# Macaron block on one Trainium2 core: the first batch's attention operands are prepared inside the first expert mixture

## The chip, the cores and the metric

The kernel runs on one NeuronCore of a Trainium2 chip, in one launch. The metric is the device time of that core in microseconds (us). SyncE (SP) and the DMA queues move data, TensorE (PE) multiplies, VectorE (DVE), ScalarE (ACT) and GpSimd (POOL) do the rest. Each engine runs its own instructions in order and waits on semaphores.

## What is computed

Four batches of 1024 rows of 128 floats pass through a feed-forward mixture, an attention and the same mixture again:

```python
x = L0_attn_x                                   # (4, 1024, 128)
x = x + 0.5 * ffn(layernorm(x))                 # first mixture
x = x + attn(layernorm(x))                      # 16 heads of 8, per batch
x = x + 0.5 * ffn(layernorm(x))                 # second mixture

# ffn: layernorm, router logits (8 experts), top 2, softmax gates, then per expert
x1 = x @ W1 + b1                                # 128 -> 512
x2 = clip(x @ W2 + b2, -20, 20)
hidden = clip(x1 * (x2 * sigmoid(x2)), -1e4, 1e4)
y = clip(hidden @ Wo + bo, -1e4, 1e4)           # 512 -> 128, summed over the 2 experts by gate
# attn: q = k = v = x @ W_qkv.T; softmax(q q^T / sqrt(8)) q; @ W_o.T
```

## The kernel before

**Mixtures.** Routing (`*_route`) ranks the experts of each row and scatters the normalised rows by expert into DRAM (`rows_dram`); the rows of an expert lie there in the order of the batches. A mixture then walks over 40 blocks: 32 "pairs" of 256 rows and at the end 8 "singles" of 128 rows, which take what is left of each expert. `vector_lay_out_early` finds the expert and the first row of blocks 0 to 16, which need the first three batches alone, `vector_lay_out_late` those of blocks 17 to 39. For every block SP loads the expert's 776 KB record of weights (`sync_load_record`, L837) and the block's rows (`sync_load_rows`, L842) into one of six slots. PE turns the rows (L1914), multiplies four chunks by W2 and W1 (L1959, L1961), DVE clips (L1689), ACT takes the Silu (L1281), DVE multiplies (L1700) and clips the whole `hidden` (L1708), PE makes the second product (L1971), ACT adds the bias (L1290), DVE clips (L1715), PE turns back (L1981), ACT weighs by the gate (L1299) and POOL scatters the result to `y_dram` (L1143). A block's steps are laid among the chunks of the next ones: in `tensor_experts` the second product of block i-1 stands between chunk 2 and chunk 3 of block i. A block's load waits until the results of the block six before are scattered (`sync_next_block`). After block 5 (first mixture) or 13 (second) SP writes eight filler rows (`sync_fillers`, L807).

**Between the first mixture and the attention.** Only when all results are scattered does SP load the first batch's results (L849, into `first_mixed`); then a table `PREPARED` of chores runs on all engines: DVE adds them to x (L1803), takes statistics (L1426, L1429), POOL the power (L1156), DVE normalises (L1818), PE turns (L2112), multiplies by W_qkv (L2118) and turns q into values (L2125), ACT copies from PSUM (L1360, L1370), DVE splits q into three bf16 parts (L1827 to L1833), SP writes them to `q_dram` (L894), SP and ACT load them as operands of the first team of four heads (L942, L1316). POOL blanks the zero parts of the operand tiles of all three operand sets and of the two value tiles in the same stretch (L1041 to L1051).

```python
PREPARED = [("prepare", 0, k, (h, 2)) for k, h in ((0, 0), (1, 0), (0, 1), (1, 1), (2, 0), (2, 1))]
```

**Attention.** Sixteen turns, one for each team of four heads of a batch. PE first makes 26 units of row-maximum scores (`tensor_row_max`, L2024, L2025; DVE reduces each, L1753). From there slots of scores (`tensor_scores`, L2043 to L2049), exponentials (ACT, L1326) and values (L2067) run, with a table `chores` that sets which other piece is issued behind which slot. Before the first score the negative row maxima must have gone through POOL (`pool_place`, L1058), DRAM (L974) and back into the right operand (L982): the chore "place" on SP, which in `sync_attention` stands behind the rows of ones of operand sets 1 and 2 (L902), the 22 loads of the second team (L942, L948, L923) and the load of batch 1's results (L883). Preparing batches 1 to 3 and the second routing are chores of the slots.

**Second mixture.** Like the first; a table `TAIL` puts the last of the attention and of the routing among its first blocks. At the end all results are loaded (`last_y`), added (L1725) and written.

## Time and profile before

| | us |
|---|---|
| median of 3 runs (1425.15 to 1428.48) | 1428.48 |
| the profiled execution, as timed | 1427.73 |
| its span, first to last instruction | 1426.0 |
| PE busy in the span | 1248.9 (88%) |
| DVE busy | 1170.2 (82%) |
| ACT busy | 896.2 (63%) |
| POOL busy | 511.2 (36%) |
| mean granted clock of TensorE | 0.964 |

The program's stages in the trace: routing to 108 us, first mixture to 331, preparing to 371, attention to 1166 (its last pieces among the second mixture's first blocks), second mixture to 1404, last sums to 1426. The busy shares are means over these stages; a stage has to be read by itself. The granted clock is given as a share of full speed: 1.0 is 2.4 GHz, 0.5 is 1.2 GHz.

### The profile page before, as it was taken

How to read it: one execution, taken by the hardware profiler on the slowest of the kernel's cores; microseconds unless marked ns; L12 is line 12 of the kernel's file. 1: busy time of each engine (PE TensorE's matmuls, PEld its weight loads, DVE VectorE, ACT ScalarE, POOL GpSimd, SP SyncE). 2: the span in 40 equal slices, each digit the busy share in tenths (PEclk: the TensorE clock that was granted, in tenths of full speed). 3: DMA queues.
4: the chain of work that ended last, by engine and by line, in shares of the span. 5: the costliest groups of instructions: out<-in, count | busy, mean ns of one | idle time of the engine just before them, and what ended most of it. 6: DMA issues, size and time to landing. Idle time of an engine off the chain costs nothing.

```text
span 1426.0 us, 29423 instructions
## 1 busy us (share of the span) xinstructions
PE 1248.9 (88%) x10053; PEld 649.7 (46%) x10053; DVE 1170.2 (82%) x2305; ACT 896.2 (63%) x1876; POOL 511.2 (36%) x595
## 2 busy tenths in 40 slices
PE   3738999984389999999999999999999988889992
PEld 3727888872022222322323323233322247778882
DVE  8876788876698899889898988988899458868885
ACT  1214555552058888888778887788877865545651
POOL 3875333334433000243335324351434023433331
PEclk9999999996589999999999999999999999999997
DMA  8126545451311201102111011011101312445555
GB/s 260 38 71 217 203 180 191 178 204 34 104 51 35 72 19 35 36 24 66 36 40 48 17 57 36 17 52 36 36 3 32 113 62 101 161 170 186 188 204 192
DMA packets 65382, 135.58 MB, mean 95 GB/s; under 512 B 13330, under 2 KB 34932, under 8 KB 65204
## 3 DMA queue, kind: packets, MB, share of 16 engines
q1 hardware_dynamic: 56196, 116.18, 23.7%
q0 software_dynamic: 8704, 16.93, 3.7%
q8 instruction: 83, 1.36, 0.4%
q14 instruction: 63, 0.52, 0.1%
q10 hardware_dynamic: 336, 0.59, 0.1%
HBM read 47.35 MB, written 25.07 MB: 51 GB/s over the span
## 4 chain that ended last, share of the span: by engine, by line
PE 44%; DVE 21%; DMA 3%; issue 3%; ACT 3%; SPq 1%; POOL 0%; ACTq 0%; POOLq 0%; DVEq 0%
PE psum L2067 13%; DVE att_neg_part L1753 11%; PE psum L2043 7%; PE psum L2047 5%; PE psum L2024 5%; PE psum L1971 3%; PE psum L1959 3%; PE psum L1961 3%; DVE att_neg_part L1758 2%; DVE stats L1426 1%; ACT att_probs L1326 1%; DMA y_dram<-ffn_y,ffn_block_rows 1%; PE psum L2090 1%; ACT att_o_t L1341 1%; DMA ffn_rec<-record 1%
## 5 line engine op out<-in xcount | busy, mean ns | idle before, releaser
L1326 ACT ACTIVATE att_probs<-psum 128x512 f32<-128x512 f32 x1024 | 556.5, 596 | 119.3 <-PE psum L2049 90.3
L1753 DVE TENSOR_REDUCE att_neg_part<-psum 128x2 f32<-128x1024 f32 x441 | 532.0, 1223 | 69.0 <-PE psum L2025 56.0
L2067 PE MATMUL psum<-att_probs,att_values 128*16 128x256 f32 x4096 | 321.4, 386 | 6.3 <-ACT att_o_t L1341 4.2
L1281 ACT ACTIVATE ffn_silu<-ffn_x2c,ffn_rec 128x256 f32<-128x256 f32 (+1 forms) x320 | 154.6, 487 | 163.3 <-DVE ffn_x2c L1689 162.6
L1143 POOL DMA_INDIRECT y_dram<-ffn_y,ffn_block_rows x144 | 142.1, 987 | 274.5 <-ACT ffn_y L1299 248.7
L2024 PE MATMUL psum<-att_right,att_left 64*128 64x512 bf16 x512 | 198.3, 388 | 27.5 <-DMA att_right<-q_parts_dram 15.9
L2043 PE MATMUL psum<-att_right,att_left 64*128 64x512 bf16 x512 | 198.6, 388 | 4.9 <-DVE att_neg_part L1753 4.8
L2046 PE MATMUL psum<-att_right,att_left 64*128 64x512 bf16 x512 | 198.5, 388 | 4.0 <-DVE att_neg_part L1753 2.1
L1689 DVE TENSOR_SCALAR ffn_x2c<-psum,ffn_rec 128x256 f32<-128x256 f32 (+1 forms) x320 | 162.8, 513 | 45.9 <-PE psum L1961 41.7
L2025 PE MATMUL psum<-att_right,att_left 64*128 64x512 bf16 x512 | 198.9, 389 | 0.0
L2047 PE MATMUL psum<-att_right,att_left 64*128 64x512 bf16 x512 | 193.7, 378 | 0.0
L2049 PE MATMUL psum<-att_right,att_left 64*128 64x512 bf16 x512 | 193.4, 378 | 0.0
L1959 PE MATMUL psum<-ffn_block_t,ffn_rec 128*128 128x256 f32 (+1 forms) x640 | 179.4, 362 | 1.3 <-ACT ffn_block_t L1239 1.1
L1961 PE MATMUL psum<-ffn_block_t,ffn_rec 128*128 128x256 f32 (+1 forms) x640 | 178.6, 361 | 0.0
L2067 PEld LDWEIGHTS psum<-att_probs,att_values 128*16 128x16 f32 x4096 | 68.1, 94 | 223.0 <-issue 125.3
L1700 DVE SCALAR_TENSOR_TENSOR ffn_hidden<-psum,ffn_rec,ffn_silu 128x256 f32<-128x256 f32 (+1 forms) x320 | 144.5, 452 | 18.9 <-ACT ffn_silu L1281 16.7
L1971 PE MATMUL psum<-ffn_hidden,ffn_rec 128*128 128x256 f32 (+1 forms) x640 | 142.6, 366 | 13.6 <-DVE ffn_hidden L1708 13.5
L1127 POOL DMA_INDIRECT rows_dram<-rows,place_i x128 | 128.5, 1004 | 72.4 <-issue 36.8
L1058 POOL TENSOR_TENSOR att_max_rest<-att_max_rest,att_max_parts 16x128 f32<-16x128 f32 x64 | 26.7, 417 | 337.4 <-ACT att_max_parts L1381 334.8
L2043 PEld LDWEIGHTS psum<-att_right,att_left 64*128 64x128 bf16 x512 | 47.4, 93 | 197.2 <-ACT att_probs L1326 125.6
L1971 PEld LDWEIGHTS psum<-ffn_hidden,ffn_rec 128*128 128x128 f32 x640 | 113.9, 193 | 32.5 <-DVE ffn_hidden L1708 18.8
L1961 PEld LDWEIGHTS psum<-ffn_block_t,ffn_rec 128*128 128x128 f32 x640 | 117.9, 192 | 13.7
(198 smaller groups left out, 1514.4 us busy)
## 6 DMA issues: line engine op xcount, KB each, us to landing
ffn_rec<-record SPq DMA_DIRECT2D x80, 776.5 KB, 3.7
ffn_block_rows<-rows_dram SPq DMA_DIRECT2D x64, 130.0 KB, 2.2
att_left<-q_parts_dram SPq DMA_DIRECT2D x64, 96.0 KB
att_right<-q_parts_dram SPq DMA_DIRECT2D x120, 48.0 KB
record<-in_L_ffn_W SPq DMA_DIRECT2D x16, 256.0 KB, 6.5
last_y<-y_dram SPq DMA_DIRECT2D x8, 512.0 KB, 7.4
att_right<-q_parts_dram SPq DMA_DIRECT2D x90, 32.0 KB
y_dram<-ffn_y,ffn_block_rows POOLq DMA_INDIRECT x144, 2.6
```

The source lines that it names most:

```text
L1326: S.activation(probs[:, slot % PROBS, :], ring_bank(("score", slot))[:, :], ACT.Exp, scale=SCALE).then_inc(att_bank.by_act, 1)
L1753: last = V.tensor_reduce(out=neg_part[:, h % 2, keys, p::PAIR, t], in_=psum[:, low:high + 1, :], axis=AX.X, op=ALU.max, negate=True)
L1959: TE.matmul(both[:, few], rec[:, s, W2 + c * P:W2 + (c + 1) * P], block_t[:, m % 2, few], start=True, stop=True)
L1961: TE.matmul(both[:, w1_few], rec[:, s, W1 + c * P:W1 + (c + 1) * P], block_t[:, m % 2, few], start=True, stop=True).then_inc(chunked, 1)
L1971: last = TE.matmul(y_bank[n % 2][:, few], rec[:, s, WO + c * F:WO + (c + 1) * F], hidden[:, n % 2, c, few], start=(c == 0), stop=(c == HC ...
L2024: TE.matmul(bank[low], left[s][TOP, p, q], right[s][TOP, p, k], start=True, stop=True)
L2025: TE.matmul(bank[high], left[s][BOTTOM, PAIR + p, q], right[s][BOTTOM, PAIR + p, k], start=True, stop=True).then_inc(maxed, 1)
L2043: TE.matmul(low, left[s][TOP, p, k], right[s][TOP, p, q], start=True, stop=False)
L2046: TE.matmul(high, left[s][BOTTOM, PAIR + p, k], right[s][BOTTOM, PAIR + p, q], start=True, stop=False)
L2047: TE.matmul(low, left[s][TOP, PAIR + p, k], right[s][TOP, PAIR + p, q], start=False, stop=True).then_inc(att_bank.filled, 1)
L2049: TE.matmul(high, left[s][BOTTOM, p, k], right[s][BOTTOM, p, q], start=False, stop=True).then_inc(att_bank.filled, 1)
L2067: last = TE.matmul(value_bank[head * VS:head * VS + VW, q], values[:, b % 2, kt, team * TEAM + head, :], probs[:, (UNIT * n + j) % PROBS, ...
```

## The change

The blocks of both mixtures are put in another order: pairs 0 to 22, then the eight singles (23 to 30), then nine pairs (31 to 39). Within each section the layout now lists first those blocks that hold rows of the first batch and then the others (16 columns of expert and half in place of 8), so that the first batch's results are complete with block 30. The layout has more small DVE instructions, and the ones over blocks are twice as wide.

In the first mixture a new table `HEAD` puts the preparing of the first batch among blocks 33 to 38, and six blanking chores among blocks 8 to 13. `plan_head(block, slots)` counts four slots to a block:

```diff
+        plan_head(BEGIN, [(HC * n, "blank", n, 0) for n in range(6)])
+        plan_head(SINGLES.stop, [
+            (8, "begin", 0, "load"), (12, "begin", 0, "add"), (13, "begin", 0, "statistics"),
+            (14, "begin", 1, "add first"), (15, "begin", 1, "add second"),
+            (16, "begin", 0, "power"), (16, "begin", 1, "statistics"), (17, "begin", 0, "normal"),
...
-        PREPARED = [("prepare", 0, k, (h, 2)) for k, h in ((0, 0), (1, 0), (0, 1), (1, 1), (2, 0), (2, 1))]
...
         def sync_next_block(k, i):
-            n = k * BLOCKS + i - SLOTS
-
-            Q.wait_ge(scattered_y[n % YSETS], y_scatters(n + 1, n % YSETS))
+            Q.wait_ge(biased, k * BLOCKS + i - SLOTS[k] + 1)
+            sync_load_record(k, i)
+            if i >= ROW_SLOTS:
+                n = k * BLOCKS + i - ROW_SLOTS
+                Q.wait_ge(scattered_y[n % YSETS], y_scatters(n + 1, n % YSETS))
             sync_load_rows(k, i)
-            sync_load_record(k, i)
+
+        def sync_first_team():
+
+            sync_ones(0)
+            sync_write_parts(0, 0)
+            sync_operand_lefts(0)
+            for n in FIRST_RIGHTS:
+                Q.dma_start(*right_load(0, n)).then_inc(first_pair_in, 16)
+            sync_write_parts(0, 1)
...
             G.wait_ge(combined, HC * BLOCKS)
             for r in range(YSETS):
                 G.wait_ge(scattered_y[r], y_scatters(BLOCKS, r))
-            pool_blank_values(0)
-            pool_blank_left(0)
-            for chore in PREPARED:
-                pool_chore(*chore)
-            pool_blank_right(0)
-            G.wait_ge(split_done, 1)
-            pool_blank_values(1)
             for s in range(1, OPERANDS):
-                pool_blank_left(s)
-                pool_blank_right(s)
+                for n in range(4):
+                    pool_blank_operands(s, n)
```

The work of the preparing is dealt out anew: POOL adds and normalises half 0, DVE half 1; ACT loads the results (`first_mixed`) and makes the three casts of each half, DVE only the subtractions; PE uses the value bank of PSUM one piece after another. SP writes the parts and loads the first team's first operands in `sync_first_team`, behind its last block load; ACT loads the others at the start of the attention. The blanking of the values and of operand set 0 is now in blocks 8 to 13, that of sets 1 and 2 stays behind the mixture. The first mixture has four record slots and the second six, both six row slots; a record waits for the bias of the block that had its slot, the rows still for the scattering of the block six before, and PE waits for the record only before the first chunk. `sync_fillers(0)` comes after block 3. The attention weights are loaded and turned with the first routing. DVE blanks the value bank after the first row maximum.

On POOL, before the change, from the first mixture's last scatters to the attention's first own step (L1058 is the first place):

```order
L1143 DMA y_dram<-ffn_y,ffn_block_rows 8448x128 x72
L1041 MEMSET att_values 128x2048
L1042 MEMSET att_values 128x128
L1046 MEMSET att_left 64x2048
L1047 MEMSET att_left 64x2048
L1156 TENSOR_TENSOR rstd<-shifted,minus_half 128x4 x2
L1050 MEMSET att_right 64x2048
L1051 MEMSET att_right 64x2048
```

The ten memsets that follow on POOL up to L1058 are those of value set 1 (two) and of operand sets 1 and 2 (four each). The same place with the change:

```order
L1232 DMA y_dram<-ffn_y,ffn_block_rows 8448x128 x34
L1124 TENSOR_TENSOR x_sb<-x_sb,att_probs 128x512 x2
L1232 DMA y_dram<-ffn_y,ffn_block_rows 8448x128 x2
L1129 TENSOR_TENSOR rstd<-shifted,minus_half 128x4
L1134 TENSOR_SCALAR att_xh<-x_sb,mean_var,rstd 128x128 x4
L1129 TENSOR_TENSOR rstd<-shifted,minus_half 128x4
L1232 DMA y_dram<-ffn_y,ffn_block_rows 8448x128 x14
L1100 MEMSET att_left 64x2048 x2
L1100 MEMSET att_right 64x2048 x2
L1100 MEMSET att_left 64x2048 x2
L1100 MEMSET att_right 64x2048 x2
L1142 TENSOR_TENSOR att_max_rest<-att_max_rest,att_max_parts 16x128
```

Eight memsets still stand between the last scatter and the first place; the others, the adds and the normalising have gone ahead of the last fourteen scatters.

On PE with the change, blocks 35 and 36 (L2081 and L2083 are the chunk's two products, L2093 the second product, L2103 the turning back, L2034 the turning of rows, L2228 turns `att_xh`, L2233 multiplies by W_qkv):

```order
L2228 MATMUL psum<-identity,att_xh 128x128 x4
L2081 MATMUL psum<-ffn_block_t,ffn_rec 128x256
L2083 MATMUL psum<-ffn_block_t,ffn_rec 128x256
L2093 MATMUL psum<-ffn_hidden,ffn_rec 128x256 x4
L2233 MATMUL psum<-att_xh_t,wqkv_t 128x512
```

Each of these was behind the whole mixture before; now chunk 2 of block 35 stands behind the turning of half 0, and chunk 3 behind its product.

On DVE with the change, blocks 34 and 35 (L1810 clips a chunk, L1821 multiplies, L1829 clips `hidden`, L1524 to L1937 are the statistics, L1932 an addition):

```order
L1829 TENSOR_SCALAR ffn_hidden<-ffn_hidden 128x1024
L1524 BN_STATS stats<-x_sb 128x6 x4
L1527 BN_AGGR mean_var<-stats 128x2 x4
L1937 TENSOR_SCALAR shifted<-mean_var 128x4
L1810 TENSOR_SCALAR ffn_x2c<-psum,ffn_rec 128x256
L1821 SCALAR_TENSOR_TENSOR ffn_hidden<-psum,ffn_rec,ffn_silu 128x256
L1932 TENSOR_TENSOR x_sb<-x_sb,att_probs 128x512
L1810 TENSOR_SCALAR ffn_x2c<-psum,ffn_rec 128x256
```

The statistics of half 0 and the first addition of half 1 now stand between the clips of block 34's chunks.

## Rows read from the trace of the kernel before

**Rows 1.** Windows: us, busy PE, PEld, DVE, ACT, POOL (count), clock, DMA share, GB/s.

```profile
332.00:371.00 39.00, 7.42 (x22) 3.76 (x22) 16.01 (x41) 3.85 (x8) 25.23 (x17) 0.54 0.24 74
371.00:420.00 49.00, 36.38 (x230) 8.72 (x234) 46.99 (x59) 16.44 (x32) 11.70 (x15) 0.65 0.26 78
420.00:700.00 280.00, 276.92 (x2816) 82.71 (x2808) 245.85 (x300) 231.00 (x449) 69.58 (x105) 1.00 0.14 41
```

**Rows 2.** Timeline of PE: start, duration; last chunk, first row maximum, first score.

```profile
326.33 0.39 PE L1961 MATMUL psum<-ffn_block_t,ffn_rec 128*128 128x128 f32 x2
...
371.11 0.60 PE L2024 MATMUL psum<-att_right,att_left 64*128 64x512 bf16 x1 [15.89 <-DMA att_right<-q_parts_dram]
...
398.87 0.63 PE L2043 MATMUL psum<-att_right,att_left 64*128 64x512 bf16 x1
```

**Rows 3.** Timelines of ACT and the chain: last weighing, last landing of results.

```profile
330.98 0.37 ACT L1299 ACTIVATE ffn_y<-psum,ffn_block_rows 128x128 f32<-128x128 f32 x1 [0.83 <-PE psum L1981]
332.12 2.10 DMA y_dram<-ffn_y,ffn_block_rows
```

**Rows 4.** Groups by form on DVE: busy us, mean ns; clip of a pair, of a single.

```profile
L1689 DVE TENSOR_SCALAR ffn_x2c<-psum,ffn_rec 128x256 f32<-128x256 f32 x256 | 137.8, 540 | 41.0 <-PE psum L1961 36.8 <-ACT ffn_silu L1281 0.5
L1689 DVE TENSOR_SCALAR ffn_x2c<-psum,ffn_rec 128x128 f32<-128x128 f32 x64 | 25.1, 405 | 4.9 <-PE psum L1961 4.9
```

**Rows 5.** Timeline of POOL: first and last of eight memsets of sets 1 and 2.

```profile
360.27 1.80 POOL L1046 MEMSET att_left<- 64x2048 bf16 x1
...
373.26 1.80 POOL L1051 MEMSET att_right<- 64x2048 bf16 x1
```

**Rows 6.** Timeline of SP's queue: second team's loads, first place.

```profile
375.73 2.35 SPq L942 DMA_DIRECT2D att_left<-q_parts_dram  x6
...
378.82 9.68 SPq L923 DMA_DIRECT2D att_right<-q_parts_dram  x14
...
393.03 0.31 SPq L974 DMA_DIRECT2D max_parts_dram<-att_max_parts  x1
```

**Rows 7.** Windows: one steady block of pairs.

```profile
226.62:232.24 5.62, 5.62 (x29) 4.95 (x28) 4.64 (x11) 3.30 (x8) 1.96 (x2) 1.00 0.45 156
```

**Rows 8.** Timelines of DVE and PE: clip of hidden, then the second product.

```profile
256.34 0.69 DVE L1708 TENSOR_SCALAR ffn_hidden<-ffn_hidden 128x1024 f32<-128x1024 f32 x1
...
257.33 0.38 PE L1971 MATMUL psum<-ffn_hidden,ffn_rec 128*128 128x256 f32 x1
```

**Rows 9.** Timelines of POOL and DVE, steady: last scatter, next clip of hidden.

```profile
242.44 0.98 POOL L1143 DMA_INDIRECT y_dram<-ffn_y,ffn_block_rows  x1 [0.31 <-issue]
...
245.10 0.69 DVE L1708 TENSOR_SCALAR ffn_hidden<-ffn_hidden 128x1024 f32<-128x1024 f32 x1
```

**Rows 10.** Groups by form: the preparing's pieces on DVE and POOL.

```profile
L1803 DVE TENSOR_TENSOR x_sb<-x_sb,att_probs 128x512 f32<-128x512 f32 x4 | 2.8, 690 | 3.2 <-DMA att_probs<-y_dram 3.1
L1426 DVE BATCH_NORM_STATS2 stats<-x_sb 128x6 f32<-128x128 f32 x8 | 1.7, 281 | 0.1
L1161 POOL TENSOR_SCALAR att_xh<-x_sb,mean_var,rstd 128x128 f32<-128x128 f32 x24 | 18.7, 789 | 0.3
```

**Rows 11.** Timelines of DVE and POOL: one normalising instruction beside a memset.

```profile
345.10 1.80 DVE L1818 TENSOR_SCALAR att_xh<-x_sb,mean_var,rstd 128x128 f32<-128x128 f32 x1
...
345.02 1.80 POOL L1050 MEMSET att_right<- 64x2048 bf16 x1
```

**Rows 12.** Waits of PE: total, times, longest; 289 to 332, then 1233 to 1405.

```profile
PE psum L1914 <- DMA ffn_rec<-record: 4.3, 2, 2.5
...
PE psum L1914 <- DMA ffn_rec<-record: 6.4, 4, 4.0
```

**Rows 13.** DVE's first clip; then PE's waits from 1166 to 1233.

```profile
111.71 0.54 DVE L1689 TENSOR_SCALAR ffn_x2c<-psum,ffn_rec 128x256 f32<-128x256 f32 x1 [5.43 <-PE psum L1961]
...
PE psum L1971 <- DVE ffn_hidden L1708: 7.0, 4, 3.1
```

**Rows 14.** Timeline of SP's queue: the fillers of the second mixture.

```profile
1243.50 11.19 SPq L807 DMA_DIRECT2D rows_dram<-filler_dram  x8
```

More of the change, by code:

```diff
@@ L244, in build_macaron @@
         first = ExitStack()
-        sets.extend(RouteSet(k, first) for k in range(1, B - 1))
-        beyond = sbuf("beyond_the_blocks", [P, 4096], owner=first)
-        sets.append(RouteSet(B - 1, first))
+        last_set = RouteSet(B - 1, first)
         VEC = 2 * E + 2 * E * HC + E
@@ L606, in build_macaron, with plan_head @@
         plan_tail([27, 29, 31], "lay", 1, 0)
+        BEGIN = 8
+        HEAD = [[] for _ in range(HC * (BLOCKS - BEGIN))]
+        def plan_head(block, slots):
+            for slot, what, which, step in slots:
+                HEAD[HC * (block - BEGIN) + slot].append((what, which, step, WHOLE))
+        plan_head(BEGIN, [(HC * n, "blank", n, 0) for n in range(6)])
[3 more added lines that the diff above has]
+            (16, "begin", 0, "power"), (16, "begin", 1, "statistics"), (17, "begin", 0, "normal"),
+            (18, "begin", 1, "power"), (18, "prepare", 0, 3), (19, "prepare", 0, 7), (20, "begin", 1, "normal"),
+            (21, "prepare", 0, 5), (21, "begin", 0, "less first"), (22, "prepare", 0, 9), (22, "begin", 0, "second part"),
+            (23, "begin", 0, "less second"), (24, "begin", 1, "less first"), (24, "begin", 0, "third part"),
+            (25, "begin", 1, "second part"), (26, "begin", 1, "less second"), (27, "begin", 1, "third part"),
+            (27, "prepare", 0, 13), (29, "prepare", 0, 15)])
         def tail(k, i, c):
+            if k == 0 and BEGIN <= i < BLOCKS:
+                return HEAD[HC * (i - BEGIN) + c]
             return TAIL[HC * i + c] if k and i < EARLY else []
@@ L661, in build_macaron @@
                 plan_banks(*chore)
-        for slot in TAIL:
+        for slot in HEAD + TAIL:
             for what, which, step, part in slot:
@@ L782, in sync_experts @@
                 sync_load_rows(0, 0)
-                for i in range(1, SLOTS):
+                for i in range(1, SLOTS[0]):
                     if i >= 2:
@@ L1073, in pool_chore @@
                 G.tensor_tensor(rows, rows, projected(half), ALU.add).then_inc(x_by_pool, 1)
+            elif what == "blank":
+                pool_blank(which)
+            elif what == "begin":
+                pool_begin(which, step)
             elif what == "mix":
@@ L1599, in vector_lay_out_late @@
+                    settle(V.tensor_tensor(skipped[:, 1, E:2 * E], ends[:, 1, E:2 * E], taken[:, :], ALU.subtract))
+                    settle(V.tensor_tensor(skipped[:, 1, E:2 * E], skipped[:, 1, E:2 * E], got[:, 0:E], ALU.subtract))
+                    settle(V.scalar_tensor_tensor(both[:, 0:E], in_pairs[:, :], -float(BH), tiles_f[:, :],
                                                   ALU.mult, ALU.add))
-                    settle(V.tensor_tensor_scan(ended[:, 2, :], unit[:, :], singles[:, :], 0.0, ALU.mult, ALU.add))
+                    settle(V.memset(both[:, E:2 * E], 0.0))
@@ L1790, in vector_chore @@
                 V.tensor_tensor(rows, rows, projected(half), ALU.add).then_inc(x_by_dve, 1)
+            elif what == "begin":
+                vector_begin(which, step)
             elif what == "prepare":
```

478 lines of the change are left out of this document (269 added, 209 removed).

## The prediction

> **What bounds the kernel now.** I read first the windows of the stages, then PE's timeline over the boundary, then the queues that stand behind it. In the 39 us behind the first mixture PE works 7.4 us, at a granted clock of 0.54, so near the lower level of 1.2 GHz after long idling, and no engine is full [rows 1]. In the next 49 us DVE is (47.0 busy: 26 units of row maxima), and from 420 us on PE (276.9 of 280 us) [rows 1]. So time taken out before the first score is gained whole, and time lost there is made up nowhere. In a mixture PE is the bound: a block of pairs takes 5.62 us and PE is busy for all of it; DVE has 4.64, which leaves it 0.98 us a block, ACT 3.30, POOL 1.96 [rows 7].
>
> The stretch to be shortened goes from the end of the last chunk (326.33 + 0.39 = 326.7) over the first row maximum (371.11, after a wait of 15.9 us for the operands) to the first score (398.87): 72.1 us [rows 2].
>
> **The boundary after the change.** Three chains end at the first score; the latest decides.
>
> First the mixture's own end. Before, the last block is a single: 331.35 - 326.7 = 4.6 us from its last chunk to its last weighing, and 334.22 - 331.35 = 2.9 us more until its scatter has landed [rows 3]. Now it is a pair. Its DVE clip takes 540 ns for 405 [rows 4]; seven steps like it and a second product of eight passes of 256 columns (some 0.1 us more each) make 1.7 us, so 6.3 us. It has two scatter issues, the second 1.3 us behind the first (taken from 0.98 and 0.31 in [rows 9]), so 4.2 us to the landing.
>
> Then the row maxima. The operands of team 0 are ready by then, I think: the last cast of q stands in the last slot of block 37; the write, eight left and six right loads at 0.69 us each (9.68 / 14 [rows 6]) and a landing take some 16 us (estimate), and two blocks and the end take 11.2 + 6.3. So row maxima begin 6.3 us after the last chunk, and the first score could follow 398.87 - 371.11 = 27.8 us later, as it did: 34.1 us.
>
> Third, what was hidden: blanking operand sets 1 and 2. These eight memsets stay behind the last scatter. They take 373.26 + 1.80 - 360.27 = 14.8 us [rows 5]; they used to run while q was being written and loaded. SP stands behind them in its order: the ones of set 2, the 22 loads of team 1, batch 1's results, and only then the first place, which the first score needs. From the end of the memsets (375.06) to the loads it took 0.67 us, the loads 12.8 (375.73 to 388.50), two more issues 1.4 (at 0.69), and from the place's first DMA to the first score 398.87 - 393.03 = 5.8 us [rows 2, 6]: 20.7 us. Before, this had 3 us to spare. Now it is 6.3 + 4.2 + 14.8 + 20.7 = **46.0 us**, 12 us later than the row maxima allow. I take 46.0: the wait for the first operands goes, and a wait of some 12 us for `max_in` takes its place. Gain: 72.1 - 46.0 = **26.1 us**. Hidden under this new wait at nothing: DVE's memset of the value bank, the eight right loads that ACT now issues late, POOL's place (its DMA went out 21.9 us after the first maximum, and the memsets now end 4.2 + 14.8 = 19.0 after it). Without that cover they would cost up to 2 us together.
>
> **The pieces among blocks 33 to 38.** On PE: sixteen turnings of 128 columns and two products of 512 columns in two passes. A block's 5.62 us at full clock is 24 passes of 256 columns and four turnings, so 0.216 us for 256 columns; the pieces are 1.7 + 1.7 = 3.5 us on the bound engine. On DVE: two additions and four subtractions at 0.69, two statistics of 1.4 (1.7 us for eight steps, so 0.85 for four, and an estimated 0.55 for what follows), four normalisings of an estimated 0.3, in all 8.2 us [rows 10], where five blocks have 4.9 us free; block 34 alone gets 2.8 us. That DVE is late matters at one edge: the clip of `hidden` ends at 257.03 and the second product starts at 257.33 [rows 8], so PE has 0.3 us there. What DVE lacks by block (2.8, 1.4, 2.6, 1.4 less 0.98 each) makes 4.5 us. To this I add waits in order: PE turns half 0 in block 35 behind POOL's four normalisings, 3.2 us [rows 10], which begin only after the last scatter and the power: about 1 us; in block 36 PE multiplies one slot after it turned half 1, and ACT copies that turn a slot late: about 1 us; clips of `hidden` that wait for POOL's adds: 1 us. PE's own pieces fall partly into these waits. I take **+8 us**, between 3.5 (PE alone) and 18 (everything one behind the other).
>
> **Blanking ahead, blocks 8 to 13.** A normalising DVE instruction beside a POOL memset took 1.80 us, its whole length [rows 11]; the clip of `hidden` is an operation of that kind (one tensor scaled, in SBUF). In a steady block POOL's last scatter issue ends at 243.42 and the next clip of `hidden` begins at 245.10 [rows 9]; a memset of 1.80 put between ends at 245.25, 0.15 us late, inside PE's 0.3. I take +0.5 us, of 0 to 9 (six times 1.5).
>
> The Trainium skill (SBUF — State Buffer, Who interferes with whom) speaks against this change: GpSimd and a DVE instruction in a two-port mode shut each other out for a whole instruction, and so do GpSimd's reads and a DVE instruction with two SBUF inputs. By that rule the additions and subtractions meet POOL's adds and normalisings too. The trace agrees for the memset; no run here shows it yet for the others.
>
> **Waits for records.** In the first mixture's singles PE waits 4.3 us for a load, in the second mixture 6.4 us: 4.0 of it behind the fillers, which hold SP for 11.2 us [rows 12, 14]. Now a record no longer waits for the scatter, nor PE's turning for the record. I take -5 us in the first mixture (with 1.5 for its fillers, which move two blocks ahead) and -7 in the second, where the clock dips after the long wait as well; ends -7 to +2 and -9 to 0.
>
> **Layout.** Some ten more small DVE instructions at 0.19 us and blocks' instructions twice as wide: +2.5 us early, +3.1 late (estimate). In the first mixture both are hidden: DVE waits 5.4 us for the first clip [rows 13], and POOL's row scatters pace the routing. In the second the late one meets a full DVE (PE already waits 7.0 us for it [rows 13]): +2.7; the early one falls into the attention: +1.2. Together +3.9, of 0 to 8. Two more changes between pairs and singles: +1.4. The second mixture too ends with a pair: (6.3 + 4.2) - (4.6 + 2.9) = +3.0.
>
> **Sum:** -26.1 + 8 + 0.5 - 5 - 7 + 3.9 + 1.4 + 3.0 = -21.3. The profiled execution took 1427.7, 0.8 below the median of the three runs, so **1406.4 us**.
>
> **Rivals.**
> 1. *No new wait at the first score.* SP or POOL get through sooner than I add up, and only the row maxima bound: 34.1 in place of 46.0. For it: it is one chain of queue order. Against it: every link has a row. 1394.5 us, chance 0.1.
> 2. *The pieces and the blanking stand in each other's way.* The rule above at work: six clips of `hidden` each 1.5 us late and the pieces 12 rather than 8: +8.5 + 4, so 1419 us. For it: the 1.80 us of [rows 11]. Against it: the gap of 1.68 us in [rows 9]. With milder forms 0.21.
> 3. *Slower: four record slots.* A record is now asked for when block i-4 has its bias, some 2.5 us after the second product of [rows 8], which is 11 us ahead of its first chunk. It decides if a record takes longer than those 11 us; each 1 us beyond costs 1 us in four blocks, 10 us over the mixture. To turn -21 into a loss it would have to take over 13.5 us; at 14 the time is 1436. Against it: a steady block moves record and rows with a DMA share of 0.45, so 2.5 us of the engines' time [rows 7]. 0.03.
> 4. *It doesn't do what it says:* the first operands come after the mixture's end. Up to 12 us of that hide under the new wait, so the time stays near my forecast; only beyond it does it count. Within the forecast.
>
> **Numbers.** Forecast 0.64 (its own range 1398 to 1415), rival 1 0.1, rival 2 0.21, rival 3 0.03, no change from what I don't see 0.02. The range reaches from rival 1 to rival 2: 1394 to 1419. A measurement of this kernel tells some 0.3% (4 us) from no change. Faster 0.94, same 0.02, slower 0.04.
>
> **What would show it.** Right: first row maximum about 6 us after the last chunk, first score about 46, PE idle some 12 us before it with SP's 22 loads in front of L1034, the eight memsets directly behind the last landing; blocks 33 to 38 together 8 us over 6 x 5.62; no wait for a load at blocks 14 and among the singles of the second mixture. Wrong: a first score 34 us after the last chunk; blocks 8 to 13 over 5.62; PE waiting on a record.

## The result, and the profile after

The changed kernel takes 1419.8 us, median of 8 runs (1417.6 to 1421.1), against 1427.6 us for the kernel before, median of 8 beside it (1424.6 to 1429.2): a ratio of 0.9947, 95% interval 0.9934 to 0.9959. It is faster by 7.8 us, where 21 were forecast, and lies 0.8 us above the range. The profiled execution's span is 1418.4 us, against 1426.0.

I cut both traces at the same events: PE's first turn of each mixture, the end of its last chunk, the first score.

| stretch (us) | before | after | difference | forecast |
|---|---|---|---|---|
| start to first mixture's first turn | 108.3 | 107.7 | -0.6 | 0 |
| first mixture, to the end of its last chunk | 218.4 | 232.9 | +14.4 | +4.2 |
| last chunk to first score | 72.2 | 48.7 | -23.4 | -26.1 |
| attention, to the second mixture's first turn | 767.3 | 769.7 | +2.3 | +1.2 |
| second mixture, to its last chunk | 232.9 | 228.3 | -4.7 | -3.6 |
| tail | 26.9 | 31.3 | +4.4 | +3.0 |

(Differences are taken before rounding. Forecast terms are put where they belong: of the changes between pairs and singles 0.7 in each mixture, of the second mixture's layout 1.2 in the attention and 2.7 behind it.) One stretch carries most of the miss, the first mixture.

**The boundary.** The timeline of PE in the kernel after (start, duration, engine and line, operation, what ended the wait before it) answers to [rows 2]:

```profile
339.93 0.59 PE L2083 MATMUL psum<-ffn_block_t,ffn_rec 128*128 128x256 f32 x2
...
347.03 0.39 PE L2140 MATMUL psum<-att_right,att_left 64*128 64x512 bf16 x1 [0.72 <-ACT ffn_y L1388]
...
389.25 0.60 PE L2159 MATMUL psum<-att_right,att_left 64*128 64x512 bf16 x1 [13.86 <-DMA att_right<-max_parts_dram]
```

The last chunk ends at 340.5 and row maxima begin 6.5 us later behind ACT's last weighing; the operands were there. The first score comes 48.7 us after the last chunk, behind 13.9 us of waiting for the place of the row maxima. POOL's memsets, in its timeline, and SP's queue answer to [rows 5] and [rows 6]:

```profile
352.58 3.65 POOL L1100 MEMSET att_left<- 64x2048 bf16 x2 [2.59 <-issue]
...
363.72 3.65 POOL L1100 MEMSET att_right<- 64x2048 bf16 x2
```

```profile
360.11 7.84 SPq L962 DMA_DIRECT2D att_left<-ones_dram  x4
368.05 2.35 SPq L1002 DMA_DIRECT2D att_left<-q_parts_dram  x6
370.45 0.65 SPq L1008 DMA_DIRECT2D att_left<-q_parts_dram  x2
...
382.37 1.47 SPq L1034 DMA_DIRECT2D max_parts_dram<-att_max_parts  x1
387.48 0.56 SPq L1042 DMA_DIRECT2D att_right<-max_parts_dram  x2
```

The chain is the forecast one: memsets, ones of set 2, 22 loads, two result loads, place. It started 12.1 us after the last chunk (forecast 10.5; the 2.59 us before it have no releaser in the profile, but in the program POOL waits there for the landing of the last scatters), and from the place's first DMA to the score it took 6.9 us (5.8).

**The first mixture.** The windows of a steady block of pairs and of five block intervals with the pieces (us, busy PE, PEld, DVE, ACT, POOL, clock, DMA share, GB/s); the first answers to [rows 7]:

```profile
220.40:226.02 5.62, 5.62 (x31) 4.95 (x30) 4.64 (x11) 3.29 (x9) 1.97 (x2) 1.00 0.51 189
292.75:329.91 37.16, 32.48 (x159) 26.31 (x158) 30.26 (x79) 21.69 (x52) 18.75 (x18) 1.00 0.48 175
```

A steady block is what it was. Five blocks with pieces take 37.2 in place of 28.1 us: 9.1 more, of which 1.3 is a wait for rows. So the pieces cost some 7.7. The rest stands elsewhere. PE's waits in its timeline, and the wait totals of 250 to 300 us (total, times, longest) that answer to the first of [rows 12]:

```profile
130.97 0.62 PE L2034 MATMUL psum<-identity,ffn_block_rows 128*128 128x128 f32 x2 [2.79 <-DMA ffn_block_rows<-rows_dram]
...
PE psum L2034 <- DMA ffn_block_rows<-rows_dram: 7.0, 6, 2.3
```

Waits for a load did not go; they changed their object, from the record to the rows, and among the singles and behind them there are 7.0 us where there were 4.3. The wait of 2.79 us at 130.97 is the one behind the fillers; the two blocks around them take 15.97 us, where the two around them took 14.13 before (+1.8). And two of the blocks with a blanking take 7.20 and 7.32 us, with 0.11 left in the next: 3.4 us over. DVE's and POOL's timelines there:

```profile
159.57 2.49 DVE L1836 TENSOR_SCALAR ffn_y_t<-ffn_y_t 128x256 f32<-128x256 f32 x1 [0.38 <-ACT ffn_y_t L1379]
...
174.21 0.29 DVE L1836 TENSOR_SCALAR ffn_y_t<-ffn_y_t 128x256 f32<-128x256 f32 x1 [0.24 <-ACT ffn_y_t L1379]
```

```profile
160.05 1.86 POOL L1094 MEMSET att_values<- 128x2048 f32 x1
161.97 0.35 POOL L1095 MEMSET att_values<- 128x128 f32 x1
...
167.38 1.84 POOL L1100 MEMSET att_left<- 64x2048 bf16 x1
...
174.75 1.80 POOL L1100 MEMSET att_left<- 64x2048 bf16 x1
```

DVE's clip of `ffn_y_t` takes 0.29 us by itself and 2.49 beside the first and second memset.

So the 14.4 us of the first mixture are 7.7 for the pieces, 3.4 for the blanking, 1.8 around the fillers and 2.7 more waiting for loads behind them, less 1.2: the changes between pairs and singles, forecast at +0.7, came out at -1.0, with 0.8 us less waiting of PE for DVE (2.0 before, 1.2 after), and the first three blocks took 0.2 less.

**The second mixture.** PE's wait totals of 1233 to 1390 us, which answer to the second of [rows 12]:

```profile
PE psum L2093 <- DVE ffn_hidden L1829: 3.4, 6, 1.8
PE psum L2034 <- DMA ffn_block_rows<-rows_dram: 2.1, 2, 1.5
```

Here waits for loads fell from 6.4 to 2.1 us, 4.3 of the 7 us that were forecast for them.

### The profile page after: what moved, and what is told of

Its sections match the earlier page's. It is cut to its first block, busy times and chain, and to the rows that moved or that the text cites. A ratio compares the mean times of both kernels' runs of the same rounds, so it can differ in the third digit from the quotient of the medians.

```text
span 1418.4 us, 29483 instructions
## 1 busy us (share of the span) xinstructions
PE 1250.7 (88%) x10053; PEld 647.6 (46%) x10053; DVE 1176.0 (83%) x2341; ACT 898.4 (63%) x1882; POOL 518.6 (37%) x603
## 3 DMA queue, kind: packets, MB, share of 16 engines
q1 hardware_dynamic: 56052, 115.39, 23.9%
## 4 chain that ended last, share of the span: by engine, by line
PE 45%; DVE 18%; issue 3%; ACT 3%; SPq 2%; DMA 2%; POOL 1%; POOLq 0%; ACTq 0%; DVEq 0%
PE psum L2183 13%; DVE att_neg_part L1869 10%; PE psum L2159 8%; PE psum L2163 5%; PE psum L2140 5%; PE psum L2093 4%; PE psum L2081 3%; PE psum L2083 3%; DVE att_neg_part L1874 1%; ACT att_probs L1403 1%; DVE stats L1524 1%; PE psum L2206 1%; ACT att_o_t L1418 1%; SPq L983 1%; PE psum L2219 1%
## 5 line engine op out<-in xcount | busy, mean ns | idle before, releaser
L2159 PE MATMUL psum<-att_right,att_left 64*128 64x512 bf16 x512 | 199.7, 390 | 20.8 <-DMA att_right<-max_parts_dram 13.9
L1810 DVE TENSOR_SCALAR ffn_x2c<-psum,ffn_rec 128x256 f32<-128x256 f32 (+1 forms) x320 | 162.2, 512 | 41.5 <-PE psum L2083 37.7
L2081 PE MATMUL psum<-ffn_block_t,ffn_rec 128*128 128x256 f32 (+1 forms) x640 | 180.4, 364 | 1.3 <-ACT ffn_block_t L1328 1.1
L2083 PE MATMUL psum<-ffn_block_t,ffn_rec 128*128 128x256 f32 (+1 forms) x640 | 179.0, 362 | 0.0
L1821 DVE SCALAR_TENSOR_TENSOR ffn_hidden<-psum,ffn_rec,ffn_silu 128x256 f32<-128x256 f32 (+1 forms) x320 | 144.1, 450 | 19.5 <-ACT ffn_silu L1370 16.9
L2093 PE MATMUL psum<-ffn_hidden,ffn_rec 128*128 128x256 f32 (+1 forms) x640 | 143.1, 367 | 15.4 <-DVE ffn_hidden L1829 15.3
L1216 POOL DMA_INDIRECT rows_dram<-rows,place_i x128 | 128.3, 1002 | 72.7 <-issue 36.8
L2159 PEld LDWEIGHTS psum<-att_right,att_left 64*128 64x128 bf16 x512 | 47.4, 93 | 214.9 <-ACT att_probs L1403 126.2
L1142 POOL TENSOR_TENSOR att_max_rest<-att_max_rest,att_max_parts 16x128 f32<-16x128 f32 x64 | 26.8, 418 | 322.2 <-ACT att_max_parts L1477 319.6
L2093 PEld LDWEIGHTS psum<-ffn_hidden,ffn_rec 128*128 128x128 f32 x640 | 112.8, 193 | 35.5 <-DVE ffn_hidden L1829 22.0
L2083 PEld LDWEIGHTS psum<-ffn_block_t,ffn_rec 128*128 128x128 f32 x640 | 118.3, 193 | 14.0
```

Source lines behind the costliest of these rows:

```text
L2081: TE.matmul(both[:, few], mix[k].rec[:, s, W2 + c * P:W2 + (c + 1) * P], mix[k].block_t[:, m % 2, few], start=True, stop=True)
L2083: TE.matmul(both[:, w1_few], mix[k].rec[:, s, W1 + c * P:W1 + (c + 1) * P], mix[k].block_t[:, m % 2, few], start=True, stop=True).then_inc ...
L2093: last = TE.matmul(y_bank[n % 2][:, few], mix[k].rec[:, s, WO + c * F:WO + (c + 1) * F], mix[k].hidden[:, n % 2, c, few], start=(c == 0), ...
L2159: TE.matmul(low, left[s][TOP, p, k], right[s][TOP, p, q], start=True, stop=False)
```

## The experiments

They ran on three other chips, on which the kernel before takes 1489 to 1499 us and the changed one 1483 to 1486 (the last section shows in which stages that time lies). Stages without those longer waits repeat there to a few hundredths: the steady block 5.62, the two blanking blocks 7.20 and 7.32. So a run's whole is read against the kernel before beside it, and the mechanism from its own stage.

**Control: the changed kernel unaltered.**

> The changed kernel unaltered, as the control on the chip of the experiments: its stages beside those of the edits. If this chip's longer times (1489 us for the kernel before, where 1428 was measured first) touch both kernels alike, the ratio is 0.995 again; its first mixture should show the two blocks of 7.2 and 7.3 us, 7 us of waits for rows among the singles and a first score 49 to 51 us after the last chunk.

1486.4 us, ratio 0.9913 (0.9885 to 0.9941). First score 51.3 us after the last chunk, blocks of 7.20 and 7.32, waits for rows as before. A second control, on a third chip:

> The changed kernel once more, beside the best version on one chip, since the earlier ratios come from different chips (0.9947, 0.9913). 0.991 to 0.995 of the kernel before, with its first score 49 to 51 us after the last chunk.

1482.8 us, ratio 0.9930 (0.9903 to 0.9957), first score at 51.2. The change is worth 0.5 to 0.9%.

**The place first.**

```diff
         def sync_attention():
+            for chore in first_chores:
+                sync_chore(*chore)
             for s in range(1, OPERANDS):
                 sync_ones(s)
             sync_operands(1)
             sync_mixed(1)
-            for chore in first_chores:
-                sync_chore(*chore)
```

> SP does the first place of the row maxima before the ones, the 22 loads of team 1 and batch 1's results; the memsets and everything else stay. Theory (the wait of 13.9 us at the first score is SP's queue order): the place's first DMA goes out about 1 us behind POOL's split instead of 13 us, the first score comes 6.9 us later or when the 26 units are through, so 36 us after the last chunk instead of 49, and the time falls by 13 us to about 1407. Rival A (the loads of team 1 are needed as early as that): row maxima of team 1 begin about 26 us after the first score and then wait, and half or more of the 13 us comes back there. Rival B (the two transfers of the place are slow in themselves): the wait stays above 10 us and the time falls by less than 3.

1480.4 us, ratio 0.9926 (0.9904 to 0.9949), not distinguishable from the controls. Yet the first score came 36.1 us after the last chunk, 15 us sooner. SP's queue:

```profile
384.75 0.31 SPq L1034 DMA_DIRECT2D max_parts_dram<-att_max_parts  x1
386.14 0.56 SPq L1042 DMA_DIRECT2D att_right<-max_parts_dram  x2
...
392.57 9.46 SPq L983 DMA_DIRECT2D att_right<-q_parts_dram  x14
402.07 0.61 SPq L943 DMA_DIRECT2D att_mixed<-y_dram  x1
```

So the wait was SP's order, as the theory said, and Rival B is out. Part of the wait was in the place's own transfers, but that too hung on the order: from the place's first DMA to its second took 1.4 us here (384.75 to 386.14), 5.1 behind the 22 loads in the kernel after and 6.3 in the first control. But the gain was given back at once, and of the 13 us expected nothing is left in the total: the first 16 calls of scores, which take 23.2 us in the kernel after (one instruction of L2159 each), took 36.8 here. PE's timeline shows the two stands, DVE's what ended the second:

```profile
404.92 0.37 PE L2140 MATMUL psum<-att_right,att_left 64*128 64x512 bf16 x1 [2.61 <-issue]
...
416.88 0.60 PE L2162 MATMUL psum<-att_right,att_left 64*128 64x512 bf16 x1 [5.08 <-DVE att_neg_part L1869]
```

```profile
414.79 0.49 DVE L1524 BATCH_NORM_STATS2 stats<-x_sb 128x6 f32<-128x128 f32 x2 [5.94 <-POOL x_sb L1170]
```

Batch 1's results, loaded last, were what POOL and then DVE stood for. The stand of 2.61 before it had no releaser in the profile.

**The place, then batch 1's results.**

```diff
             for chore in first_chores:
                 sync_chore(*chore)
+            sync_mixed(1)
             for s in range(1, OPERANDS):
                 sync_ones(s)
             sync_operands(1)
-            sync_mixed(1)
```

> As the run with the place first, but with batch 1's two results loaded right behind the place, ahead of the ones and the 22 loads of team 1. In that run the first score came 14 us sooner and the whole was given back within 37 us: DVE stood 5.9 us for POOL's addition of batch 1's results, whose load now went out behind the 22. Theory: with them ahead this wait goes, the first 16 scores take at most 28 us instead of 36.8, and at least 8 of the 14 us stay: 8 us below the changed kernel. Rival A: the 22 loads of team 1 are what is late, and their wait takes the same place: nothing gained. Rival B: what stood there was the engine's own issue (2.6 us of it was shown so), which the 14 us of waiting had covered: 4 to 6 us gained.

1479.6 us, ratio 0.9866 (0.9835 to 0.9896), 6.8 us below its control. DVE's stand was gone; the first 16 calls took 32.4 us, more than the 28 of the theory, and 6.8 lies between the 8 of the theory and the nothing of Rival A, so the total alone picks none. PE's stand grew, with SP's last load of team 1 (14 from 395.63) issued by 405.2:

```profile
408.18 0.58 PE L2140 MATMUL psum<-att_right,att_left 64*128 64x512 bf16 x1 [5.99 <-issue]
```

In both runs this stand ended 2.9 to 3.0 us after the last of the 14 right loads was issued, and it is at the row maxima that first use team 1's operands (behind 26 units before the first score and one more behind each call, the 33rd unit comes between the seventh and the eighth call of scores; the expectations below count it as the ninth). That speaks for the loads, as in Rival A, over Rival B, though the profile names nothing.

**The place between the loads.**

```diff
-            for s in range(1, OPERANDS):
-                sync_ones(s)
-            sync_operands(1)
-            sync_mixed(1)
+            sync_mixed(1)
+            sync_ones(1)
+            sync_operand_lefts(1)
+            for n in range(8):
+                Q.dma_start(*right_load(1, n)).then_inc(rights_in[1], 16)
             for chore in first_chores:
                 sync_chore(*chore)
+            for n in range(8, RIGHT_LOADS):
+                Q.dma_start(*right_load(1, n)).then_inc(rights_in[1], 16)
+            sync_ones(2)
```

> SP's order behind the mixture: batch 1's two results, the ones of set 1, the eight left and eight of the 14 right loads of team 1, the first place, the other six right loads, the ones of set 2. In the two runs with the place first the first score came 15 us sooner, and PE then stood 6 to 8 us at the first unit of team 1 (the ninth call of scores), 2 to 3 us behind the last of its 22 loads. Theory (both ends hang on SP's order of issue): the loads now run while the memsets of set 2 do, so the first score comes 35 to 37 us after the last chunk and the ninth call of scores 22 to 24 us behind the first score as in the changed kernel (11.7 at the ninth), with no wait over 1 us between: 13 to 15 us below the changed kernel. Rival (the stand of 6 us is the engine's own issue, covered by the wait before): it comes again at the same place in the program, and only 7 us are gained.

1468.5 us, ratio 0.9849 (0.9825 to 0.9874). SP's queue:

```profile
375.14 5.94 SPq L919 DMA_DIRECT2D att_right<-q_parts_dram  x8
381.15 0.40 SPq L1038 DMA_DIRECT2D max_parts_dram<-att_max_parts  x1
384.04 0.56 SPq L1046 DMA_DIRECT2D att_right<-max_parts_dram  x2
384.64 3.96 SPq L923 DMA_DIRECT2D att_right<-q_parts_dram  x6
```

First score at 34.7 us, the first 16 calls in 25.5 us, no stand at team 1's first unit: it was the loads. From the last chunk to the second mixture it took 847.4 us, against 859.2 in the run with the blanking edit on the same chip (whose boundary is the changed kernel's): 11.8 us gained, less than the 13 to 15 expected, of the 16 by which the first score is earlier. Of what is given back 3.1 us stand in the first 16 calls (25.5 for 22.4 in that other run). PE's windows of 6 us from the first score, of this run and of the kernel after.

```profile
387.00:393.00 6.00, 5.75 (x27) 1.16 (x25) 5.59 (x7) 3.25 (x6) 0.00 (x0) 0.50 0.43 113
393.00:399.00 6.00, 6.00 (x60) 1.35 (x54) 4.58 (x4) 3.39 (x7) 0.00 (x0) 0.82 0.29 71
```

```profile
389.25:395.25 6.00, 6.00 (x40) 1.68 (x40) 3.89 (x5) 3.63 (x7) 3.08 (x3) 0.61 0.41 109
395.25:401.25 6.00, 6.00 (x69) 1.56 (x61) 5.75 (x7) 5.11 (x11) 0.00 (x0) 1.00 0.18 62
```

With no wait before the first score the granted clock is 0.50 (the level of 1.2 GHz) and 0.82 in these windows, and DVE, still full with row maxima, is busy for 5.59 of the first 6 us; in the kernel after it is 0.61 and 1.00, and DVE 3.89. In both the clock has been 0.50 since well before the first score (in the kernel after from 351 us on, with PE busy for 2.7 of 5 us). How the 3.1 us divide between the clock and DVE is not shown.

**Rows before records.**

```diff
-            Q.wait_ge(biased, k * BLOCKS + i - SLOTS[k] + 1)
-            sync_load_record(k, i)
             if i >= ROW_SLOTS:
                 n = k * BLOCKS + i - ROW_SLOTS
                 Q.wait_ge(scattered_y[n % YSETS], y_scatters(n + 1, n % YSETS))
             sync_load_rows(k, i)
+            Q.wait_ge(biased, k * BLOCKS + i - SLOTS[k] + 1)
+            sync_load_record(k, i)
```

> From the block behind the four (six) slots on, SP loads a block's rows before its record, behind the scatter alone, in both mixtures. Theory (rows come late because SP holds them back behind the record's wait for the bias of block i-4): the waits of PE for rows among the singles of the first mixture, 7.0 us in six places, fall below 2 us, and the time falls by about 5 us to 1415. Rival (the transfers themselves are late: 776 KB of records and the rows share one queue, and four record slots are too few for singles of 3 us): the waits turn into waits for records of the same size, 5 to 9 us, and the time stays within 2 us.

1471.1 us, ratio 0.9873 (0.9833 to 0.9914), the lowest of the four that ran on its chip together. Waits of PE from 250 to 308 us, in this run:

```profile
PE psum L2034 <- DMA ffn_block_rows<-rows_dram: 1.5, 2, 1.1
```

Waits for rows fell to 1.5 us (6.6 and 6.7 in the two controls), and PE's waits name no record in their place. One wait of 0.46 us before a first chunk has no releaser in the profile; a record may be behind it, but not the 5 to 9 us of the rival. From the turn of block 24 to that of block 39 it took 78.9 us, against 81.9 in the run with the place first on the same chip: 3.0 of the 5 expected. The other 2 came back in the next block, which took 8.27 us in place of 6.38: PE there waited 1.2 us for the clip of `ffn_y_t` and 0.7 for DVE's product (L1821), on a DVE that stood 1.2 us behind POOL's addition. In the changed kernel the wait for rows had covered part of that.

**The fillers spread.**

```diff
-                sync_fillers(0)
             for i in range(SLOTS[k], EARLY):
                 sync_next_block(k, i)
-                if k == 1 and i == 13:
-                    sync_fillers(1)
+                if k == 0 and 5 <= i < 5 + E:
+                    sync_fillers(0, i - 5, i - 4)
+                if k == 1 and EARLY - 4 <= i:
+                    sync_fillers(1, 2 * (i - EARLY + 4), 2 * (i - EARLY + 5))
```

(`sync_fillers` takes the first filler and the stop.)

> The eight filler writes of the first mixture go out one by one behind the loads of blocks 5 to 12 instead of all behind block 3's; those of the second in pairs behind the loads of blocks 13 to 16. Theory (they hold SP for 11 us, and only that makes a block's rows late): in the first mixture the block of 8.6 us and the one of 7.4 us behind it become 5.62, -4.7 us; in the second the 7.27 at block 14 becomes 5.62 too, -1.6 us; together 6 us, to about 1413.5. Rival (the rows of block 4 are late because the scatters of the routing are): the wait of 2.8 us stays and the time falls by 2 us at most.

1476.3 us, ratio 0.9902 (0.9864 to 0.9941). In PE's timeline blocks 4 and 5 now turn without a wait, and the second mixture's block 14 takes 5.62:

```profile
136.54 0.38 PE L2035 MATMUL psum<-identity,ffn_block_rows 128*128 128x128 f32 x2
142.16 0.38 PE L2035 MATMUL psum<-identity,ffn_block_rows 128*128 128x128 f32 x2
147.78 0.38 PE L2035 MATMUL psum<-identity,ffn_block_rows 128*128 128x128 f32 x2
```

So the theory holds for these places. Its size is less sure: the two intervals of blocks 4 and 5 take 11.2 us here and 12.7 to 16.5 in the four runs of that chip that keep the fillers together (15.97 in the kernel after), and the 1.4 to 1.6 us of block 14 don't show in the second mixture's length, 232.6 us for 232.4, since the two blocks around its early layout took 25.9 for 23.9. The intervals of the whole times overlap, so the 6 us expected are not shown.

**Each blanking behind the clip.**

```diff
         def pool_blank(n):
+            G.wait_ge(y_clipped, BEGIN + n)
```

> Each of the six blankings among blocks 8 to 13 waits until DVE's clip of ffn_y_t of the block before is done. Theory (a memset and that clip shut each other out: it took 2.49 us beside the memset twice and 0.29 elsewhere): all six blocks take 5.62 us, no clip over 0.6 us, and the time falls by 3.3 us to about 1416.5. Rival (the two blocks are long for another reason, such as the rows or a clock that has just come back): they stay at 7.2 and 7.3 us and the time does not move; or another DVE instruction takes the 1.8 us in place of the clip.

1476.9 us, ratio 0.9918 (0.9894 to 0.9943); the whole is too coarse for 3.3 us. The stage is not: the three intervals of 7.20, 7.32 and 5.73 are 5.62, 5.62 and 5.68, so 3.3 us are back. POOL's and DVE's timelines:

```profile
190.47 1.80 POOL L1100 MEMSET att_left<- 64x2048 bf16 x1 [0.78 <-DVE ffn_y_t L1837]
```

```profile
190.12 0.29 DVE L1837 TENSOR_SCALAR ffn_y_t<-ffn_y_t 128x256 f32<-128x256 f32 x1 [0.37 <-issue]
```

A memset held back by 0.8 us costs PE nothing. One clip of `hidden`, at 181.01 beside the end of the first memset, takes 0.89 us for 0.69, in the block of 5.68; no other instruction is held for a memset's length.

**The pieces a slot later.** The diff of the table of slots, its first lines:

```diff
-            (8, "begin", 0, "load"), (12, "begin", 0, "add"), (13, "begin", 0, "statistics"),
-            (14, "begin", 1, "add first"), (15, "begin", 1, "add second"),
+            (8, "begin", 0, "load"), (12, "begin", 0, "add"), (14, "begin", 0, "statistics"),
+            (15, "begin", 1, "add first"), (16, "begin", 1, "add second"),
...
-            (27, "prepare", 0, 13), (29, "prepare", 0, 15)])
+            (28, "prepare", 0, 13), (30, "prepare", 0, 15)])
```

> The pieces of DVE, ACT and PE for batch 0 one slot (a quarter of a block) later: the statistics of half 0 to slot 14, the rest behind it, the first turn on PE to slot 19, the last copy to slot 30; POOL's stay. Theory (part of the 8 us are waits in order, DVE 1.2 us behind POOL's addition and PE 1.4 us behind POOL's normalising): the blocks that take 6.4 and 8.5 us lose 2 to 3 us together, and the time falls by 2 to 3 us; the row maxima still begin 6.5 us after the last chunk, since the operands had some 6 us to spare. Rival (the pieces cost by their own length, and where they stand doesn't matter): under 1 us; or the operands come late and row maxima begin later than 8 us after the last chunk, hidden under the wait for the place.

1483.1 us, ratio 0.9902 (0.9875 to 0.9929). The four intervals behind the wait for rows took 5.74, 9.20, 6.92 and 6.41, together 28.3 us; in the control of the same chip 6.35, 9.07, 8.56 and 6.55, so 30.5; in another run there 30.0. That is 1.8 to 2.3 us, and of PE's waits the one for POOL's normalising went (1.9 us in that control, 1.4 in the kernel after). So about a quarter of the pieces' 7.7 us was waiting in order. The whole time, 3.3 us under the control, doesn't show it by itself, since the intervals overlap. Row maxima began 7.9 us after the last chunk, against 8.2 in the control: the operands still came in time.

**All together.**

> All five edits: the place and batch 1's results first, rows before records, the fillers spread, each blanking behind DVE's clip, the pieces a slot later. If each removes a wait of its own on the path, they add up: 8 to 13 (place) + 3 (rows) + 5 (fillers) + 3.3 (blanking) + 2.5 (pieces) = 22 to 27 us below the changed kernel, so a ratio of 0.977 to 0.980 to the kernel before. If they share waits (rows that are early let the pieces wait instead, as in the run with the rows first), 15 to 20 us.

1468.4 us, ratio 0.9794 (0.9768 to 0.9819): 18.0 us below its control, in the lower of the two bands, that of shared waits. With the place between the loads:

> That order with the four other edits (rows before records, fillers spread, blanking behind DVE's clip, pieces a slot later). The five together gave 0.9794 of the kernel before, where the changed kernel gave 0.9913. Theory: the wait at team 1's first unit goes, 7 us more: 0.974 to 0.976. Rival (that wait is not the loads'): 0.979 as before.

1456.8 us, ratio 0.9774 (0.9750 to 0.9798), a little above the band; its interval overlaps that of the run before it, on another chip, so this pair alone doesn't decide. The same kernel beside the changed one on one chip:

> The version with all edits, unaltered, beside the changed kernel: if its stages keep what they showed (first mixture 13 to 14 us shorter, first score 13 to 15 us sooner after the last chunk, of which 2 to 4 come back at the low clock of the attention's first scores, the second mixture 1.5 us shorter), it is 22 to 26 us below the changed kernel on the same chip; if part of that was the difference between chips, 15 to 20.

1456.0 us, ratio 0.9757 (0.9732 to 0.9783), where the changed kernel takes 1482.8: **26.8 us less**, a little more than the 22 to 26 expected. By stretch: first mixture 233.4 us for 245.5, last chunk to second mixture 849.7 for 862.4, second mixture 233.0 for 235.9. This version beats both kernels.

## Why the prediction was wrong

**Right.** The removed wait for operands, and a new one in its place: 46.0 us were forecast from last chunk to first score, 48.7 came, with the 12 us of idling (13.9) where they were forecast, and SP's loads as its cause, which moving the place showed. The 2.7 us more are a landing of the last results 1.6 us later and a place that took 1.1 longer. Right in size too: the pieces (+8 forecast, 7.7 measured), with waits in order as a part of it (the run with later pieces); the late layout hidden in the first mixture. The second mixture came near its forecast (-3.6, measured -4.7) in part by luck: waits for loads gave 4.3 us of the 7, the two blocks around the layout cost 2.2 (2.7 forecast), and the 2.6 us that make up the rest had no term in the forecast; no run takes them apart. Rival 3 is out: in no run with the change do PE's waits name a record. (By its own rate its loss would begin at 13.1 us for a record, not 13.5, and what DVE lacks by block adds up to 4.3 us, not 4.5; neither slip matters to the forecast.)

**The step that failed: "-5 us in the first mixture" for the waits for records.** Measured are +4.5: 1.8 for the fillers and 2.7 more waiting among the singles and behind them, so the miss is 9.5 of the 13.8 us between the forecast and the profiled execution. (The 1.5 us for the fillers stand in the prediction without a sign. A sum of -5 against 4.3 us of waits that had a row fits a saving; moving them two blocks ahead cost 1.8.) The step took away the record's wait for the scatter and PE's wait for the record at the turn, and did not ask what is late next. It is the rows: in SP's queue they stand behind the record, and the record waits for the bias of the block *four* back instead of the scatter of the block six back. SP's own waits from 244 to 290 us (total, times, longest) show it standing before the record, and hardly before the rows:

```profile
SPq L904 <- ACT ffn_y_t L1379: 17.3, 10, 3.2
SPq L909 <- DMA y_dram<-ffn_y,ffn_block_rows: 1.4, 1, 1.4
```

So the rows go out later than their own six slots allow. In SP's queue rows were issued here:

```profile
257.98 1.40 SPq L910 DMA_DIRECT2D ffn_block_rows<-rows_dram  x1
```

The next turn that waited stood 2.26 us for rows, until 262.49. In steady pairs of 5.62 us nothing waits, in singles of 3 to 3.5 us four blocks are too short a time. (One wait stands in a pair, 1.34 us at 299.88, though its rows were issued at 293.42; what held them is open, but it too was gone with the rows ahead.) Putting the rows ahead took all but 1.5 us of these waits away (5.1 to 5.5 us). In the second mixture the same order stands with six slots, and there waits for loads fell by 4.3 us.

**A term mis-sized: blanking ahead, +0.5, measured 3.4.** I weighed the memset against the clip of `hidden`, which it lengthened in three blocks by only 0.1 us, inside PE's 0.3, and not against the clip of `ffn_y_t`, which in the kernel before runs from 242.91 to 243.20, just where POOL's last scatter ends (243.42). It was the milder part of rival 2. The rule of the Trainium skill (SBUF — State Buffer, Who interferes with whom), that GpSimd and a DVE instruction in a two-port mode shut each other out for a whole instruction, agrees with these two clips of 2.49 us, and the run with the wait shows it by removing them. The same section says that a DVE instruction with two SBUF inputs contends with GpSimd's reads as well, which was my reason to give rival 2 its 0.21. A hold for a whole instruction did not show there: DVE's addition beside POOL's normalising took 0.77 us, where the one before it took 0.68.

```profile
305.86 0.77 DVE L1932 TENSOR_TENSOR x_sb<-x_sb,att_probs 128x512 f32<-128x512 f32 x1
```

```profile
305.54 3.31 POOL L1134 TENSOR_SCALAR att_xh<-x_sb,mean_var,rstd 128x128 f32<-128x128 f32 x4
```

The forecast by rival 2, 1419, lies near the result for a reason it did not have: it had 8.5 us for six clips and 4 more for the pieces, and the loads were no part of it. That is luck.

**Smaller.** The tail is +4.4 for +3.0: in the second mixture's end the last product of eight passes took 2.87 us where it takes 1.99 at the boundary of the first; the granted clock over it was 0.67, and 1.00 at the boundary:

```profile
1389.64 2.87 PE L2093 MATMUL psum<-ffn_hidden,ffn_rec 128*128 128x256 f32 x8 [1.79 <-DVE ffn_hidden L1829]
```

The attention is +2.3 for +1.2, with one wait of 3.17 us for a row maximum at 1071, where the early layout of the second mixture lies; no run takes that apart, so its cause is open.

## What to carry to other kernels

When a load gets fewer slots, look at every load that is issued behind it in the same queue, and at the shortest blocks, not the mean one: the wait moves to them. A new wait that serves as a cover can hide several things at once (here the loads of team 1, batch 1's results and DVE's backlog of row maxima), so before its removal is counted as a gain, the queue behind it has to be put in the order in which the transfers are needed. Work that is moved beside a mixture should be weighed against each instruction that may lie next to it, and held back by a semaphore where it would start beside one that it can block: 0.8 us of holding a memset back saved 1.6 us in each of two blocks.

## What the runs showed of the hardware

A memset on POOL held a DVE instruction that had begun, by the profile, 0.48 us before it (159.57 and 160.05), by 2.2 us, until 0.15 us after the memset's end; the second pair (166.89 and 167.38) is alike. At a distance of 0.54 us (174.21 and 174.75) it did not. In its usual 0.29 us the clip would have been over at 159.86, before the memset's recorded start, so the recorded starts don't show when the hold began. An addition of POOL, which reads, lengthened a clip of `hidden` by 0.11 us only (0.80 for 0.69).

A transfer of the place took 1.4 us when it was issued ahead of 22 loads on SP's queue, and 5.1 to 6.3 when it was issued behind them.

The other three chips take 61 to 71 us more for the kernel before and 63 to 67 for the changed one. In the second control 42 of them are in the attention (811.2 us for 769.7) and about 13 in the first mixture, in its first blocks. In the attention they are stands at the same three places of the program in every run there, 355 to 377, 563 to 591 and 711 to 743 us after the first score, and ACT's waits of over 2.4 us add up to 30 to 39 us; the kernel after had one of 3.8. In the second control PE and ACT stand at the first of these places while POOL issues its 16 scatters of rows one behind the other. ACT's timeline and PE's:

```profile
760.66 1.08 ACT L1403 ACTIVATE att_probs<-psum 128x512 f32<-128x512 f32 x2 [3.68 <-remote]
770.50 0.60 ACT L1403 ACTIVATE att_probs<-psum 128x512 f32<-128x512 f32 x1 [8.76 <-remote]
```

```profile
761.40 0.58 PE L2140 MATMUL psum<-att_right,att_left 64*128 64x512 bf16 x1 [3.09 <-issue]
...
771.25 0.58 PE L2140 MATMUL psum<-att_right,att_left 64*128 64x512 bf16 x1 [6.82 <-issue]
```

On the first chip the same scatters are in the 50 us from 730, and PE is busy for 49.2 of them; here it is busy for 38.4 of the 50 us from 750. The scatters themselves take 0.96 us each on both. What ACT stood for is not named in the profile and was not tried, so the cause is open. The ratio of one and the same change was 0.9947 on the first chip and 0.9913 and 0.9930 on two others; the intervals overlap, so a difference between the chips in it is not shown.
